# A cross-attention kernel: TensorE makes a step's value products ahead of the step's second group of projection slices

## What is computed

```python
q = _split_heads(query @ Wq.T + bq, B, Q)
k = _split_heads(key @ Wk.T + bk, B, KV)
v = _split_heads(value @ Wv.T + bv, B, KV)
scores = jnp.einsum('bhqd,bhkd->bhqk', q, k) / SCALE
top_scores, top_idx = jax.lax.top_k(scores, eff_k)          # eff_k = 32
w = jax.nn.softmax(top_scores, axis=-1)
out = jnp.einsum('bhqk,bhqkd->bhqd', w, top_v)
return out @ Wo.T + bo
```

## Time and profile before

| | before |
|---|---|
| median of 3 runs | 2188.55 us (2187.51 to 2192.39) |
| profiled execution | 2197.32 us, span of its trace 2195.5 us |
| TensorE busy (matmuls) | 1952.2 us, 89% of the span |
| VectorE busy | 1822.8 us, 83% |
| ScalarE busy | 1302.9 us, 59% |
| GpSimd busy | 1269.3 us, 58% |

### The profile page before, as it was taken

How to read it: one execution, slowest core, us unless ns; L and a number is a source line. 1 busy time by engine, 2 the same in 40 slices (tenths; PEclk the granted TensorE clock), 3 DMA queues, 4 the chain that set the end, 5 groups by cost and what they waited for, 6 DMA issues and landing times.

```text
span 2195.5 us, 49817 instructions
## 1 busy us (share of the span) xinstructions
PE 1952.2 (89%) x19472; PEld 1518.1 (69%) x19472; DVE 1822.8 (83%) x3413; ACT 1302.9 (59%) x2600; POOL 1269.3 (58%) x1533
## 2 busy tenths in 40 slices
PE   5999999999987889899889889988989988988965
PEld 3666656665664778687777777777868777777753
DVE  6676766667634799999999999998999999999893
ACT  4333333333323577677678678767777867876852
POOL 5565646464623365656557656666665655765642
PEclk9999999999988999899999999999999999999977
DMA  6000000000135110101002002011010100200100
GB/s 205 13 13 24 13 24 13 24 13 21 34 128 139 32 50 14 39 19 50 24 17 67 19 22 54 14 40 47 22 33 22 53 21 20 66 20 21 36 1 12
DMA packets 51108, 82.35 MB, mean 38 GB/s; under 512 B 9741, under 2 KB 26381, under 8 KB 50874
## 3 DMA queue, kind: packets, MB, share of 16 engines
q1 hardware_dynamic: 46442, 71.70, 11.1%
q0 software_dynamic: 2672, 4.19, 1.0%
q10 hardware_dynamic: 1760, 3.28, 0.5%
HBM read 60.59 MB, written 9.86 MB: 32 GB/s over the span
## 4 chain that ended last, share of the span: by engine, by line
PE 39%; ACT 12%; POOL 7%; issue 6%; DVE 3%; DMA 1%; POOLq 1%; SPq 1%; ACTq 0%; another core or an unknown queue 0%; DVEq 0%
PE ca_pF L88 6%; PE ca_pF L90 6%; PE ca_pF L89 6%; PE ca_pO L1332 3%; PE ca_pT L1282 3%; ACT ca_W L1443 3%; PE ca_pX L1390 3%; PE ca_pX L1381 3%; PE ca_pS L88 2%; POOL ca_QL L1151 2%; PE ca_pS L89 2%; PE ca_pS L90 2%; ACT ca_S L1461 2%; ACT ca_S L1453 1%; ACT ca_top L1446 1%
## 5 line engine op out<-in xcount | busy, mean ns | idle before, releaser
L1684 DVE MATCH_REPLACE8 ca_W<-ca_top,ca_W 128x722 f32<-128x722 f32 x600 | 535.8, 906 | 0.0
L1674 DVE MAX8 ca_top<-ca_W 128x8 f32<-128x722 f32 x600 | 518.7, 909 | 0.8
L1117 POOL TENSOR_TENSOR ca_S<-ca_S,ca_W 128x722 f32<-128x722 f32 x200 | 344.8, 1746 | 101.6 <-ACT ca_W L1443 101.6
L1096 POOL TENSOR_TENSOR ca_KL<-ca_K,ca_KH 128x384 fp32r<-128x384 f32 (+1 forms) x128 | 122.8, 959 | 212.5 <-ACT ca_KH L1436 206.6
L1665 DVE MAX8 ca_top<-ca_S 128x8 f32<-128x722 f32 x200 | 175.6, 911 | 73.4 <-ACT ca_S L1461 56.6
L88 PE MATMUL ca_pF<-ca_cH,ca_WkH 128*128 128x338 f32 (+1 forms) x512 | 190.1, 371 | 22.9 <-POOL ca_cL L1104 12.7
L88 PE MATMUL ca_pS<-ca_KH,ca_QH 128*128 128x362 f32 (+1 forms) x384 | 146.0, 380 | 70.8 <-ACT ca_S L1461 64.1
L1470 ACT ACTIVATE ca_PT<-ca_pT 128x768 f32<-128x768 f32 x200 | 161.6, 808 | 56.0 <-PE ca_pT L1282 52.7
L335 POOL TENSOR_TENSOR sa_ss<-sa_ss,sa_minus_half 100x16 f32<-100x16 f32 x64 | 189.6, 2979 | 7.2 <-DVE sa_ss L515 7.2
L1453 ACT ACTIVATE ca_S<-ca_S,ca_shift 128x722 f32<-128x722 f32 x200 | 169.2, 894 | 36.1 <-POOL ca_shift L1110 35.8
L1443 ACT ACTIVATE ca_W<-ca_W,ca_shift 128x722 f32<-128x722 f32 x200 | 179.8, 899 | 15.0 <-DVE ca_W L1684 15.0
(11 more groups left out here) (224 smaller groups left out, 5034.5 us busy)
## 6 DMA issues: line engine op xcount, KB each, us to landing
ca_raw<-in_ctxT SPq DMA_DIRECT2D x32, 384.0 KB, 4.0
ca_raw<-in_ctxT SPq DMA_DIRECT2D x32, 338.0 KB, 3.0
ca_RKH<-ca_KH SPq DMA_DIRECT2D x64, 90.2 KB, 2.1
ca_RKL<-ca_KL SPq DMA_DIRECT2D x64, 90.2 KB, 2.2
sa_xin<-in_x SPq DMA_DIRECT2D x16, 200.0 KB
sa_xres<-in_x SPq DMA_DIRECT2D x16, 200.0 KB
x_scratch<-sa_x SPq DMA_DIRECT2D x16, 200.0 KB
x_scratch<-y_scratch POOLq DMA_DIRECT2D x16, 200.0 KB, 13.9
```

The source lines that it names most:

```text
L1117: pool.tensor_tensor(S[k][:, :], S[k][:, :], W[r][:, :], ALU.subtract).then_inc(p_ready, 1)
L1674: n_of[t.i] = order.mark(dve.max(top[r][:, 8 * k:8 * k + 8], W[r][:, :]))
L1684: ins = dve.match_replace(W[r][:, :], eight, W[r][:, :], REMOVED)
```

## The change

In TensorE's `body` the call of `values` moves up by a few lines: from the end of the step to a place ahead of the second group of slices.

```diff
@@ -1381,6 +1381,8 @@
                             pe.matmul(pX[0:T, :], ctxT[:, c, :], WoT[:, c, :], start=c == 0, stop=False)
                         pe.wait_ge(xb_ready, b.count(1, 0))
                         pe.matmul(pX[0:T, :], ident[0:T, 0:T], x2[:, :], start=False, stop=True).then_inc(y_mm, 1)
+                    if len(old) > 1:
+                        values(*old)
                     for x in slices(s, 1, b, par, tiles, nxt):
                         project(*x)
                     if s == 1 and nxt:
@@ -1395,8 +1397,6 @@
                         transposed(xin, x2T_mm)
                     if s == 5 and tiles and not b.const % 2:
                         rest_score(bn, 1 - par, scored(b, NT))
-                    if len(old) > 1:
-                        values(*old)
             each_batch(pe, body)
```

## The result

The changed kernel takes 2293.53 us (median of four runs, 2292.67 to 2294.46) against 2190.3 us for the kernel before on the same chip: ratio 1.0468, 95% interval 1.0452 to 1.0484. That is 103 us slower; the prediction said 45 us, with a range up to 2260. The sign and the chain were right, the size was not.

The account below looks back on a forecast made before the run. ScalarE's copies in program order, for which TensorE waits, were taken to set the pace, with VectorE trailing. Delays at five kinds of place summed to 45.3 us over the median 2188.55, giving 2234 us, range 2215 to 2260.

Parts of the forecast that it names:

- the chain: Late last slice on TensorE delays ScalarE's slice copy, context rounding, weight copy and score copy, for which TensorE waits.
- The terms of the order: Delays from the moved block at the ends of steps 0 and 3 and even steps 4 to 6: 45.3 us.
- Step 3: Way into step 4: 1.14 us late in 7 odd batches, 1.43 us in 8 even ones.
- step 0: Way into step 1: 0.90 us late in even and 1.49 us in odd batches, 7 times each.
- Even steps 4 to 6: Block before three slices delays GpSimd's chain to the query's low part: 1.15 us, 8 times.
- steps 1 and 2: ScalarE copies the second slice group later but makes it good in the following step: zero counted.
- the wait for the score copy: TensorE's wait for ScalarE's L1461, said to grow by 1 to 1.5 us each as a sign of being right.
- the rival: Longer waits at two places make TensorE's clock fall more often: 7 x 1.7 us more, 2246 us; chance 0.09.
- Busy times stay: Sign of being right: the engines' busy times in a pair of batches do not change.
- the block would fill waits: Rival: block costs nothing in odd step 4 and even step 5, 20 us less, 2169 us; chance 0.07.
- VectorE would take the lag up: Rival: VectorE sets the pace and its idle time absorbs the lag, no change, 2189 us; chance 0.06.
- The wait of the block for L1470: Sign of being wrong: if the moved block waits over 1 us for the weight copy, places are dearer.

Follow-up runs that it names:

- equal fillers: Kernel before given exactly the changed kernel's table of unneeded matmuls in TensorE's waits, 2191.56 us (1.0008); the changed kernel with that table took 2228.59 us (1.0160).

## Why the prediction was wrong in size

**The bound and the chain: right.** ScalarE's program order sets the pace, VectorE trails. The rows of after show the late slice, L1421 and L1470 behind it without a gap, and VectorE's longer waits; the run with ScalarE made late shows that lateness there costs time without the block being moved (24 us for 0.57 us a step).

**The terms of the order: right in sum.** 45.3 us were predicted; 33 to 47 us are measured at a high clock, and 5.4 to 7.0 us a pair for 6.1. Step 3 (19.4 for 18) and step 0 (16.7 for 18) hold. Even steps 4 to 6 were taken at 9.2, 1.15 a time; the medians give 2 us, the pairs at a clock of 1.00 1.0 to 1.2 a time, and the wait for the query grew by 1.3 (2.01 us against 0.71). Nothing is then left for steps 1 and 2, where the prediction had zero. Where the lag shows was read wrongly at one place: in odd step 4 not the wait for the score copy grew but a new one of 1.15 us stands ahead of it.

**The clock: the step that failed.** The prediction wrote "I add nothing for it to the sum", and priced the rival at one more fall of 1.7 us in each odd batch, 12 us, with a chance of 0.09. The runs show 56 us (70 with equal fillers). The mis-sizing has a cause that the rows of before could have shown in part. The prediction looked for new falls only at the two waits that were long already, and set against the rival that "falls that are there cannot come again". But its own terms lengthen short waits: the context's of 1.59 us, the query's of 0.71 and NR's of 0.54, each followed by a clock of 1.00 before. Adding 1.43, 1.15 and 1.49 to them gives 3.0, 1.9 and 2.0 us, about the length (2.12) of the wait behind which the clock was at 0.62. Three new falls in each pair were a possibility to be priced, some 1.5 to 1.7 us each by the spells that were there. How many would come, these rows could not tell: 1.65 us of idle time was followed by none, and after the change the context's 3.0 us were followed by one in half of the cases. The Trainium skill, "TensorE: Matmul & The Clock Gate", Part 1, on which the rival leant, points the right way: idle time brings the lower level back. The trace agrees in 14 of 17 cases: of the waits for the context, the query and NR between 900 and 1990 us after the change, 14 are followed by a mean clock of 0.57 to 0.73 over 4 us and three by 1.00; before, when they were shorter, all are followed by 1.00.

**"Busy times stay": wrong,** for the same reason: TensorE's rose by 5 to 9 us a pair. VectorE's idle time in a pair, predicted to go from 9 to 15 us, went to 20 and 23.

**The other rivals.** That the block would fill waits or that VectorE would take the lag up did not happen. The wait of the block for L1470, named as what would make places dearer if it passed 1 us, did so once in a pair (1.3 in even step 5, which the prediction counted as part of the 1.15) and averaged 0.6 in the 24 cases of the table.

## What to carry to other kernels

A wait that grows can cost twice on TensorE: its own length, and a slower stretch behind it where the clock stayed up before. So add the lag to every wait on the path, not only to the long ones, and look up in the stretches of the trace which waits are followed by a clock under 1, in several pairs, since one and the same wait can have it in one pair and not in the next. In this kernel, work that nobody needs soon was better kept where it stood, behind work that others copy out. And before an order is judged, fillers cut to the waits of both kernels, or pairs at the same clock, tell the order's price from the clock's.

## What was not expected of the hardware

Matmuls that compute nothing made the kernel before faster: 2178.85 us with fillers of its own waits, 0.5% under it. With more of them than the waits hold the gain is gone (2191.56 with the table made for the longer waits). And a clock of 1.00 from 900 to 1990 us could be had with idle times of up to 1.3 us left in it: the value block's wait in even step 5 of the changed kernel with fillers is still 1.32 us.
